# A mesh product in high and low parts, and all attribute columns among the layers: one graph network kernel on one core

## The reference

```python
def _L0_gnn_ref(x, Ws_self, Ws_neigh, bs, src, dst):          # three layers
    h = x
    for l in range(3):
        neigh = segment_sum(h[src], dst, num_segments=n) * inv_deg
        h = h @ Ws_self[l] + neigh @ Ws_neigh[l] + bs[l]
        if l != 2:
            h = relu(h)
    return h

def _L1_gnn_ref(grid_nfeat, mesh_nfeat, edge_index, efeat, ...):
    e = _mlp(efeat, emb_...)                                   # 4 attributes -> 512
    e_in = concatenate([e, mesh_nfeat[src], grid_nfeat[dst]], -1)
    e_new = _mlp(e_in, edge_...) + e
    agg = segment_sum(e_new, dst, ...)
    return _mlp(concatenate([grid_nfeat, agg], -1), node_...) + grid_nfeat

x = _layernorm(x + _L0_gnn_ref(x, ...))
x = _layernorm(x + _L1_gnn_ref(x, mesh_nfeat, edge_index, edge_attr_4, ...))
```

## Time and profile before

| | |
|---|---|
| median of 3 runs | 2257.26 us (2256.71 to 2258.75) |
| the profiled execution's own time | 2256.75 us |
| its span (first to last instruction) | 2255.0 us |
| granted TensorE clock, mean of the span | 0.992 |
| PE busy | 2190.3 us, 97% |
| DVE busy | 1502.7 us, 67% |
| ACT busy | 1218.0 us, 54% |
| POOL busy | 1206.8 us, 54% |
| DMA | 149.81 MB, mean 66 GB/s |

### The profile page before, as it was taken

The page is one execution under the profiler, slowest core; times in us unless marked ns, Lnnn a source line. Parts: engine busy times, 40 slices in busy tenths (PEclk is TensorE's granted clock), DMA queues, the critical chain, the costliest instruction groups (busy, mean ns, idle before and its releaser), DMA issues. The chain is left out here.

```text
span 2255.0 us, 44895 instructions
## 1 busy us (share of the span) xinstructions
PE 2190.3 (97%) x13039; PEld 1881.9 (83%) x13040; DVE 1502.7 (67%) x3372; ACT 1218.0 (54%) x2244; POOL 1206.8 (54%) x1721
## 2 busy tenths in 40 slices
PE   7999989999999999999999999999999999999898
PEld 4367888888789989899898998989989989889776
DVE  8425975344756777767767667766776676767666
ACT  2221114333256676677666767667667667667421
POOL 0775028885535555565555555555555555555223
PEclk9999999999999999999999999999999999999899
DMA  6421001112363333323332333333323332333131
GB/s 203 127 56 41 0 6 40 8 40 54 114 210 88 64 62 63 62 60 65 60 65 61 65 60 65 63 63 60 65 60 60 65 65 61 60 65 65 27 92 44
DMA packets 81814, 149.81 MB, mean 66 GB/s; under 512 B 20523, under 2 KB 20989, under 8 KB 81754
## 3 DMA queue, kind: packets, MB, share of 16 engines
q0 software_dynamic: 47248, 93.38, 21.5%
q1 hardware_dynamic: 34505, 55.67, 7.8%
HBM read 128.90 MB, written 19.71 MB: 66 GB/s over the span
## 5 line engine op out<-in xcount | busy, mean ns | idle before, releaser
L1667 ACT ACTIVATE b_bank<-c_bias 128x512 f32<-128x512 f32 x528 | 316.4, 599 | 15.1 <-PE b_bank L1779 10.0
L145 POOL DMA_INDIRECT s_attrs<-k_attrs,k_row_i x170 | 224.4, 1320 | 168.0 <-POOLq L2233 117.2
L1600 DVE CUSTOM_DVE_ANT_0 b_bank<-b_bank,c_p,k_floor 128x512 f32<-128x512 f32 x176 | 132.5, 753 | 255.5 <-PE b_bank L1801 254.6
L1445 POOL DMA_INDIRECT c_from_src<-s_dst_table,c_at_nodes x173 | 278.5, 1610 | 32.2 <-issue 32.2
L1856 PE MATMUL b_bank<-k_m_hi,c_pt_hi 128*128 128x512 f32 x704 | 293.8, 417 | 0.0
L1432 POOL DMA_INDIRECT c_from_src<-s_mesh_table,c_at_nodes x176 | 202.3, 1149 | 152.3 <-POOL c_at_nodes L1428 142.5
L1857 PE MATMUL b_bank<-k_m_lo,c_pt_hi 128*128 128x512 f32 x704 | 277.9, 395 | 0.0
L1451 POOL TENSOR_TENSOR c_dev<-c_var,k_half 128x1 f32<-128x1 f32 x176 | 99.3, 564 | 327.5 <-DVE c_var L1582 327.5
L1858 PE MATMUL b_bank<-k_m_hi,c_pt_lo 128*128 128x512 f32 x704 | 273.9, 389 | 0.0
L1738 ACT ACTIVATE c_h<-c_from_src 128x512 f32<-128x512 f32 x176 | 111.3, 632 | 263.4 <-DVE c_from_src L1621 263.4
L1799 PE MATMUL b_bank<-c_m_hi,c_ht_hi 128*128 128x384 f32 x704 | 222.5, 316 | 6.3 <-DVE c_ht_lo L1587 6.0
(11 more groups left out here) (352 smaller groups left out, 5859.9 us busy)
## 6 DMA issues: line engine op xcount, KB each, us to landing
c_from_src<-s_mesh_table,c_at_nodes POOLq DMA_INDIRECT x176
c_from_src<-s_dst_table,c_at_nodes POOLq DMA_INDIRECT x173, 4.7
s_attrs<-k_attrs,k_row_i POOLq DMA_INDIRECT x170
a_mesh<-in_L_gnn_mesh_nfeat_dram SPq DMA_DIRECT2D x10, 224.0 KB
k_h<-in_x_dram SPq DMA_DIRECT2D x10, 224.0 KB
s_mesh_table<-a_mesh_out SPq DMA_DIRECT2D x10, 224.0 KB
b_x<-in_x_dram SPq DMA_DIRECT2D x10, 224.0 KB
s_node_own<-b_out SPq DMA_DIRECT2D x10, 224.0 KB
```

The costliest lines, as they stand in the source:

```text
L145: return pool.indirect_dma_start(scratch["attrs"], bass.IndirectOffsetOnAxis(ap=k["row_i"][0:EP, c:c + 1], axis=0), k["attrs"][0:EP, A4 * ...
L1445: pool.indirect_dma_start(from_src[u][:], None, scratch["dst_head" if head else "dst_table"], bass.IndirectOffsetOnAxis(ap=at_nodes[u][:, ...
L1600: dve.tensor_tensor_reduce(var1_bank[:], var1_bank[:], p[u % 2][:], 1.0 / D, k["floor"][:, 0:1], ALU.mult, ALU.add, var[u][:, 0:1]).then_i ...
L1667: act.activation(bank[:], bias[:, m, :], ACT.Copy).then_inc(bank_set, 1)
```

## The change

- The mesh product is made as three products of high and low parts, 12 matmuls a tile by `product` in place of 4 in float32. `w0b_hi` (by ACT, after the second row) and `w0b_lo` (by DVE, written over `w0b`) are new, as are `mesh_lo` (by DVE, over `wnb`) and `mesh_low` for each tile.
- PE turns tile n + 2 right after it has multiplied tile n, and the loops of the mesh stage are written out on PE, DVE, ACT and SP.
- The mesh tiles from the third on are loaded by ACT (`mesh_load`), after its copy of the tile that had the buffer.
- SP loads the first bias before the mesh stores, not after them.
- The 24 attribute columns of phase a move to phase b: its first block has 154 columns.

```diff
-ATTR_EARLY, ATTR_LATE, ATTR_PAIR = 24, 16, 4
+ATTR_LATE, ATTR_PAIR = 16, 4
...
+    w0b_hi = Region(nc, W0A_AT, SBUF_END)("a_w0b_hi", [P, KC, D], F32R)
+    w0b_lo = Region(nc, W0B_AT, SBUF_END)("a_w0b_lo", [P, KC, D], F32R)
+    late_low = Region(nc, WNB_AT, SBUF_END)
+    mesh_lo = [late_low(f"a_mesh_lo{i}", [P, KC, P], F32R) for i in range(2)]
...
     def _(sp):
...
-        with sp.Fori(0, NB // 2 - 1) as i:
-            for u in range(2):
-                sp.wait_ge(mesh_turned, 2 * i + u + 1)
-                move_rows(sp, mesh[u][:], node_rows(t["L1_gnn_mesh_nfeat"], 2 * i + 2 + u), mesh_in[u])
-            for u in range(2):
-                sp.wait_ge(mesh_ok, 2 * i + u + 1)
-                move_rows(sp, node_rows(scratch["mesh_table"], 2 * i + u), mesh_out[u][:], mesh_stored[u])
-        for u in range(2):
-            n = NB - 2 + u
+        sp.dma_start(bias0[:], rows(t["L0_gnn_bs"][0]).broadcast_to([P, D])).then_inc(bias_in, 16)
+        for n in range(NB):
             sp.wait_ge(mesh_ok, n + 1)
-            move_rows(sp, node_rows(scratch["mesh_table"], n), mesh_out[u][:], mesh_stored[u])
-
-        sp.dma_start(bias0[:], rows(t["L0_gnn_bs"][0]).broadcast_to([P, D])).then_inc(bias_in, 16)
+            move_rows(sp, node_rows(scratch["mesh_table"], n), mesh_out[n % 2][:], mesh_stored[n % 2])
...
     def _(pool):
...
-        for c in range(ATTR_EARLY):
-            scatter_attr(pool, scratch, k, c).then_inc(attr_scattered[c // BACKLOG % 2], 16)
         open_gates(pool, 1)
-        for u in range(2):
-            pool.wait_ge(attr_scattered[u], 16 * batched(ATTR_EARLY, u))
...
     def _(dve):
...
+        def mesh_low(n, u, fixed):
+            dve.wait_ge(mesh_t_ok, n + 1)
+            if not fixed:
+                dve.wait_ge(mesh_mm, n - 1)
+            dve.tensor_tensor(mesh_lo[u][:, :, 0:NPB], spread(bank[4 + u]), mesh_t[u][:, :, 0:NPB].bitcast(F32),
+                              ALU.subtract).then_inc(mesh_lo_ok, 1)
+
+        dve.wait_ge(w0b_hi_ok, 1)
+        dve.tensor_tensor(w0b_lo[:], w0b[:], w0b_hi[:].bitcast(F32), ALU.subtract).then_inc(w0b_ok, 1)
         for u in range(2):
-            mesh_copy(u, u, True)
...
+            mesh_low(u, u, True)
+        for n in range(NB):
+            mesh_copy(n, n % 2, n < 2)
+            if n + 2 < NB:
+                mesh_low(n + 2, n % 2, False)
+            if n in (2, 4):
+                i = n // 2 - 1
+                dve.wait_ge(w_hi_ok, i + 1)
+                dve.tensor_tensor(w_lo[i][:], w[i][:], w_hi[i][:].bitcast(F32), ALU.subtract).then_inc(w_lo_ok, 1)
...
     def _(act):
...
+            if r == 1:
+                act.activation(w0b_hi[:], w0b[:], ACT.Copy).then_inc(w0b_hi_ok, 1)
...
+        def mesh_load(n):
+            act.wait_ge(mesh_turned, n - 1)
+            move_rows(act, mesh[n % 2][:], node_rows(t["L1_gnn_mesh_nfeat"], n), mesh_in[n % 2])
+
         for u in range(2):
             mesh_copy(u, u, True)
+            mesh_load(2 + u)
...
     def _(pe):
...
-                pe.wait_ge(mesh_t_ok, n - 1)
+                pe.wait_ge(mesh_lo_ok, n - 1)
...
-            for c in range(KC):
-                last = pe.matmul(bank[6 + u][0:NPB, :], mesh_t[u][:, c, 0:NPB], w0b[:, c, :], start=(c == 0), stop=(c == KC - 1))
-            last.then_inc(mesh_mm, 1)
+            left = (lambda c: mesh_t[u][:, c, 0:NPB], lambda c: mesh_lo[u][:, c, 0:NPB])
+            product(pe, bank[6 + u][0:NPB, :], left, (lambda c: w0b_hi[:, c, :], lambda c: w0b_lo[:, c, :]),
+                    range(KC)).then_inc(mesh_mm, 1)
...
-        for u in range(2):
-            multiply(u, u, True)
-        with pe.Fori(1, NB // 2) as i:
-            for u in range(2):
-                turn(2 * i + u, u, False)
-            for u in range(2):
-                multiply(2 * i + u, u, False)
+        for n in range(NB):
+            multiply(n, n % 2, n < 2)
+            if n + 2 < NB:
+                turn(n + 2, n % 2, False)
...
-        columns = EC - ATTR_EARLY
-        scatter(0, columns - ATTR_LATE)
+        scatter(0, EC - ATTR_LATE)
```

More of the change, by code:

```diff
@@ L120 @@
 SORT_AT, TEMP_AT, FOLD_AT, SBUF_END = 87296, 112128, 132864, 229344
+W0A_AT, WNB_AT, W0B_AT = (FOLD_AT + n * KC * D * 4 for n in (6, 7, 8))
 SUMS_AT, LATE_AT, AGG_AT, U_AT, SPARE_AT = 24768, 90624, 104192, 179968, 220928
@@ L224, in phase_a @@
     mesh = [fd(f"mesh{i}", [NPB, D]) for i in range(2)]
-    mesh_t = [fd(f"mesh_t{i}", [P, KC, P]) for i in range(2)]
+    mesh_t = [fd(f"mesh_t{i}", [P, KC, P], F32R) for i in range(2)]
     mesh_out = [fd(f"mesh_out{i}", [NPB, D]) for i in range(2)]
+    w0b_hi = Region(nc, W0A_AT, SBUF_END)("a_w0b_hi", [P, KC, D], F32R)
+    w0b_lo = Region(nc, W0B_AT, SBUF_END)("a_w0b_lo", [P, KC, D], F32R)
+    late_low = Region(nc, WNB_AT, SBUF_END)
+    mesh_lo = [late_low(f"a_mesh_lo{i}", [P, KC, P], F32R) for i in range(2)]
     h, w = keep["h"], [keep["w0"], keep["w1"]]
@@ L245, in phase_a @@
     scattered = [sem(f"scattered{i}") for i in range(2)]
-    attr_scattered = [sem(f"attr_scattered{i}") for i in range(2)]
     pairs_in, pairs_read, pairs_turned = sem("pairs_in"), sem("pairs_read"), sem("pairs_turned")
@@ L681, in _ @@
             act.activation(w_hi[i][:], w[i][:], ACT.Copy).then_inc(w_hi_ok, 1)
+            mesh_copy(2 + i, i, False)
+            mesh_load(4 + i)
         def copy_h(n):
@@ L689, in _ @@
             copy_h(n)
-        with act.Fori(1, NB // 2) as i:
-            for u in range(2):
-                mesh_copy(2 * i + u, u, False)
+        for n in range(4, NB):
+            mesh_copy(n, n % 2, False)
+            if n + 2 < NB:
+                mesh_load(n + 2)
         def high(n):
@@ L789, in multiply @@
         def multiply(n, u, fixed):
-            pe.wait_ge(mesh_t_ok, n + 1)
-            if not fixed:
+            pe.wait_ge(mesh_lo_ok, n + 1)
+            if fixed:
+                pe.wait_ge(w0b_ok, 1)
+            else:
                 pe.wait_ge(mesh_ok, n - 1)
-            for c in range(KC):
-                last = pe.matmul(bank[6 + u][0:NPB, :], mesh_t[u][:, c, 0:NPB], w0b[:, c, :], start=(c == 0), stop=(c == KC - 1))
-            last.then_inc(mesh_mm, 1)
+            left = (lambda c: mesh_t[u][:, c, 0:NPB], lambda c: mesh_lo[u][:, c, 0:NPB])
+            product(pe, bank[6 + u][0:NPB, :], left, (lambda c: w0b_hi[:, c, :], lambda c: w0b_lo[:, c, :]),
+                    range(KC)).then_inc(mesh_mm, 1)
         for u in range(2):
             turn(u, u, True)
-        for u in range(2):
-            multiply(u, u, True)
-        with pe.Fori(1, NB // 2) as i:
-            for u in range(2):
-                turn(2 * i + u, u, False)
-            for u in range(2):
-                multiply(2 * i + u, u, False)
+        for n in range(NB):
+            multiply(n, n % 2, n < 2)
+            if n + 2 < NB:
+                turn(n + 2, n % 2, False)
         def turn_h(n):
@@ L1017, in _ @@
             if i % 2 and left > 0:
-                scatter(columns - left, columns - left + ATTR_PAIR)
+                scatter(EC - left, EC - left + ATTR_PAIR)
                 if left == ATTR_PAIR:
                     for u in range(2):
-                        pool.wait_ge(attr_scattered[u], 16 * batched(columns, u))
+                        pool.wait_ge(attr_scattered[u], 16 * batched(EC, u))
                     pool.dma_start(k["attrs"][:], scratch["attrs"].rearrange("(p t) a -> p (t a)", p=P)).then_inc(attrs_in, 16)
```

9 lines of the change are left out of this document (3 added, 6 removed).

## The result

The changed kernel takes 2262.62 us, the median of 17 runs (2259.93 to 2265.65). The kernel before, timed together with it, takes 2259.15 (17 runs). The ratio is 1.0017, with a 95% interval of 1.0009 to 1.0024. Of 2259 us that is +3.8 us (+2.0 to +5.4). The middle is under the 0.2% (4.5 us) that I had named as the bound, the upper end of the interval over it; the time is inside the range of 2252 to 2268. The forecast was +2.7.

A forecast was written before the change was run, and what follows sets the result against it. PE, busy for 97% of the span, was taken as the bound, with VectorE setting the pace in some stages. -7.6 - 7.4 + 17.7 = +2.7 us on 2256.75; forecast 2259.6 us, range 2252 to 2268.

The forecast's parts named there:

- part two: Counting loop: with 24 early columns out of the first block, slow tiles 4 to 7 vanish, 7.4 us earlier.
- Part one: Mesh stage: high and low part products replace float32 matmuls on PE, stage ends 7.6 us earlier.
- Part three: Second block: the 24 columns, now ahead of POOL's first power, make VectorE and PE wait, 17.7 us later.
- the loop's entry is slow by itself: Rival at the counting loop's start: part two gives nothing, sum +10.1, 2267 us; chance 20%.
- the lock in full: Rival in the second block: POOL and VectorE's two-SBUF-input instructions fully exclude each other, delay 21.8, sum +6.8, 2264 us; 8%.

The follow-up runs named there:

- E1: Changed kernel with the 24 early attribute columns back in the first block, so mesh product and bias only, chip A: 2257.69 us, ratio 0.9998 to the kernel before.
- E9: The kernel before, unchanged, traced again on chip B: ratio 1.0003, counting 115.85 us.
- E3: Changed kernel with 12 attribute columns early and 142 ahead of the first power, chip A: 2245.51 us, ratio 0.9940 to the kernel before.
- E4: Kernel before with 36 early attribute columns in place of 24, chip A: 2270.40 us, ratio 1.0050 to the kernel before.
- E2: Kernel before with only the 24 early columns moved to the second block, chip A: 2269.73 us, ratio 1.0051 to the kernel before.
- E11: Changed kernel with 12 attribute columns early, on chip B: 2246.03 us, ratio 0.9971 to the kernel before.
- E7: Changed kernel with 120 POOL memsets in place of the 24 early columns and all gates opened by SP: 2340.22 us, ratio 1.0391 to the kernel before.

## Why the prediction was right

The terms and their mechanisms came out as said, up to the points below. That their sum did is in part luck: one of the three terms, part two, hangs on a condition that I did not know of.

**Part one, -7.6.** The stage gave -7.71, in every kernel that has the new product: 33.55 us. The start of the first product (2.04 us behind the first turn), the 3.23 us a tile and the loads in time came as worked out. What I took for a term of its own wasn't one. On chip A the mesh part alone is worth nothing (E1). I wrote that the early columns end at 207.35 whatever the loop does, and didn't draw from it that an earlier loop meets more of them. The sum holds because both parts are in the change.

**Part two, -7.4.** Measured -8.10, 0.5 outside my bound of 7.6. I counted the slow tiles 4 to 7 and VectorE's wait; the tiles behind them were slower too, VectorE waiting for PE once at 211.05. PE's granted clock is low there (a mean of 0.80 from 208 to 216, where E9 has 1.00), which fits, but was not tried by itself. That the slow stretch ends with POOL's columns is borne out by E1, E3 and E4 on chip A. That POOL's columns are enough to make it is refuted by E9. The rival "the loop's entry is slow by itself" falls too: the changed kernel, E2 and E3 enter at full pace. (One of my arguments against it was misread: rows 2, from 149 to 155, stand beside the scatter of the edges and not beside the early columns, which begin at 171.83.) The cause needs the columns and a second condition, which held in E1 and E4 on chip A and in no trace on chip B. What it is stays open.

**Part three, +17.7.** Measured +18.27, in E2 +17.2. The one-to-one passage, PE's pause and the clock without cost came as said. Of my two estimates for the 24 columns, 37.4 us (1.49 each and a stretch of 1.6 beside VectorE) and 38.6 (1.61 each, the mean of the block), the first was right. In the changed kernel the 130th column starts at 520.33 and the 154th at 557.56, so the last 24 took 37.23 us, a stretch of 1.47. The rest of the miss is the first 130 columns, which took 0.54 us longer, and the start of the block, 0.21 later behind the last count.

How the stretch comes about I had wrong: it is not a quarter of VectorE's time. Here are a column and the subtraction beside it (POOL, then VectorE):

```profile
531.16 2.19 POOL L146 DMA_INDIRECT s_attrs<-k_attrs,k_row_i  x1 [0.30 <-issue]
530.80 1.48 DVE L1058 TENSOR_TENSOR b_a_lo<-k_adj,b_a_hi 125x1280 fp32r<-125x1280 int16 x1
```

The column starts 1.12 us before the subtraction ends and takes 1.00 us more than its 1.19. In phase b of this trace 28 columns start inside a VectorE operation with two SBUF inputs, at least 0.2 us before its end, and each takes the rest of that operation, less 0.12 to 0.13 us, in addition. A column that has started 0.15 us or more before such an operation loses at most 0.15 us, and the subtractions `L1058` keep their 1.47 to 1.49 us. With the lock in full for all of VectorE's time it would have been 21.8. The Trainium skill's rule (SBUF — State Buffer, "SBUF: two separate sides") gives the ports to whichever comes first, for the whole instruction, and in the case of two SBUF inputs only against a GpSimd operation that reads SBUF. This trace agrees where the subtraction came first, and shows no such block where the column did.

**What the sum lacked.** Stages of the changed kernel against before: -7.48 up to the zero matmuls, -8.10, +18.27, and +1.62 in the edges, together +4.3 where the ratio says +3.8. The forecast of +2.7 is as near as that because part two gave 0.7 more than I had, which makes up for half of the edges' 1.6. (From the first mesh turn to the end the two traces are 5.6 us apart; the other 1.3 are 0.3 between the first power and the edges and 1.0 behind the edges.) I had nothing for the edges, which the diff doesn't touch. In all eight traces with the new mesh product they take 1446.1 to 1446.7 us, in all six without 1444.5 to 1444.7. POOL's gather from the mesh table is what differs in the page's groups, E9 and then E11:

```profile
L1432 POOL DMA_INDIRECT c_from_src<-s_mesh_table,c_at_nodes x176 | 202.3, 1149 | 152.3 <-POOL c_at_nodes L1428 144.1
```

```profile
L1451 POOL DMA_INDIRECT c_from_src<-s_mesh_table,c_at_nodes x176 | 210.3, 1195 | 148.9 <-POOL c_at_nodes L1447 139.8
```

Whether the longer gathers cost the 1.9 us wasn't tried, nor why they are longer. E7 speaks against it: its gathers have a mean of 1161 ns, a quarter of the way from 1149 to 1195, and its edges still take 1446.08 us. The cause of this term is open.

**On chip B** I would expect the change to be slower, an estimate from the table: -7.5 - 1.0 + 18.3 + 1.6 = +11 us, 0.5%. It wasn't run there.

**A slip.** The time that the prediction names, 2259.6 us, doesn't follow from its own sum: 2259.45 and the 0.5 us from the profiled execution to the median are 2260.0. It changes nothing in the comparison.

## What to carry to other kernels

An engine that is idle in a trace has room for as much work as its idle time, and the end of the room is sharp: 12 of 24 moved columns were free, the other 12 cost their full length, because the next job of that in-order engine was waited for. Gains in neighbouring stages don't add up where one stage's length decides how much of another it meets; run each part alone before you credit it. And a loss seen in one trace may belong to where that trace was taken: trace the unchanged kernel again, on another chip, before you build on it.

## What the runs showed of the hardware

- A stream of short memsets on POOL held up one VectorE instruction (88x256 int32, SBUF to SBUF) from 182.93 to the stream's end, 12.48 us in place of 0.28 (E7). POOL started a memset every 0.18 us, each 0.25 us long and behind a wait for the last but one, so that in the record two overlap at any time. That the stream held the instruction up is inferred from its end, which comes with the stream's. VectorE's operations that read PSUM ran beside the same stream at their usual 0.69 us. The Trainium skill (SBUF — State Buffer, "Who interferes with whom") has GpSimd and a VectorE operation that takes the shared ports block each other for one instruction; here some seventy memsets went by before VectorE had its turn.
- A column that starts during one of VectorE's subtractions of two SBUF tiles takes the rest of the subtraction, less 0.12 to 0.13 us, in addition (28 of 28 in the changed kernel's phase b); one that started 0.15 us or more before loses at most 0.15 us.
- Beside POOL's columns SP's loop of gates went at 1.56 us a pass in the first trace and at 1.49 in E1, and at 1.14 in E9, on chip B.
- PE's pause of 17.67 us brought its granted clock to 0.50 until 565, and the stage behind lost nothing by it, VectorE being its bound.
- The same program counted its tiles in 122.99 us in one execution and in 115.85 in another, on chip B, with POOL's columns at the same place. On chip B the medians of the same kernel held to 0.4 us (2251.79 and 2252.18).
- Two DMA issues on ScalarE take 0.77 us, largely beside its copy, where four on SP took 1.99.
